# A graph network's third layer: the pass that scores the edges goes on in eight strands, its q rows spread by two wide operations a step

## What is computed

```
q = (x @ Wq_w + Wq_b)[dst]                       # per edge, by target node
k_base = (x @ Wk1)[src] + k_rel[edge_type] + Wk_b
score_base = sum(q * k_base, axis=-1)
scores = (score_base[:, None] + q @ v_rule.T) * scale      # E x 4
... softmax over edges of one (type, target), mean over rules: attn_mean
proj = einsum('nd,rdo->nro', x, W_r)             # 6250 x 32 x 128
msg = proj[src, edge_type] * attn_mean[:, None]
out = segment_sum(msg, dst) + bias
```

## Time and profile before

| what | us |
|---|---|
| timed runs | 8304.05, 8308.06, 8335.11 (median 8308.06) |
| profiled execution | 8250.15, span of its instructions 8248.4 |
| VectorE busy over the span | 3976.9 (48%) |
| GpSimd busy over the span | 5188.7 (63%) |
| TensorE, ScalarE busy | 893.5, 698.3 |
| line 2110, the gathers of this pass | 781.4 busy, 387.6 idle before them |

### The profile page before, as it was taken

One profiled execution on the slowest core, in us unless ns is written; L12 is line 12 of the kernel. 1 busy time (PEld: TensorE's weight loads), 2 busy tenths in 40 slices (PEclk: granted clock), 3 DMA queues, 4 the chain that ended last, 5 costly groups with the idle time before them and its releaser, 6 DMA issues. The chain is left out here.

```text
span 8248.4 us, 28229 instructions
## 1 busy us (share of the span) xinstructions
PE 893.5 (11%) x3512; PEld 557.4 (7%) x3512; DVE 3976.9 (48%) x9781; ACT 698.3 (8%) x1673; POOL 5188.7 (63%) x5178
## 2 busy tenths in 40 slices
PE   7500000000000000000025654000000001000000
PEld 5500000000000000000012221000000001000000
DVE  8974456023434443343335666666333335454536
ACT  0021111000000010000013332000000003000002
POOL 0067763766767657677755666662767766676774
PEclk9999755555555555555557887555555555555555
DMA  2080001013333323232225776331323331333332
GB/s 49 1 325 2 2 1 25 15 20 84 95 95 99 96 88 107 85 103 88 90 79 184 260 247 213 105 104 38 93 85 93 95 95 54 85 102 87 100 87 65
DMA packets 302982, 771.14 MB, mean 93 GB/s; under 512 B 125644, under 2 KB 135938, under 8 KB 289482
## 3 DMA queue, kind: packets, MB, share of 16 engines
q0 software_dynamic: 166224, 282.97, 14.8%
q1 hardware_dynamic: 118356, 375.36, 12.4%
q10 hardware_dynamic: 18210, 111.02, 3.5%
HBM read 357.59 MB, written 411.37 MB: 93 GB/s over the span
## 5 line engine op out<-in xcount | busy, mean ns | idle before, releaser
L1797 POOL DMA_INDIRECT first_sj<-scores,first_atdst x784 | 799.6, 1020 | 690.9 <-POOLq L59 430.9
L846 POOL DMA_INDIRECT l2z_rows<-proj,l2z_idx x784 | 791.6, 1010 | 427.5 <-issue 242.5
L2110 POOL DMA_INDIRECT l2s_krow<-table_k,l2s_idx x784 | 781.4, 997 | 387.6 <-issue 263.3
L846 POOL DMA_INDIRECT l3z_rows<-table,l3z_idx x784 | 797.5, 1017 | 327.1 <-issue 236.7
L846 POOL DMA_INDIRECT l1z_rows<-table,l1z_idx x784 | 783.4, 999 | 333.1 <-issue 241.5
L846 POOL DMA_INDIRECT l0z_rows<-table,l0z_idx x784 | 773.2, 986 | 331.0 <-issue 233.9
L822 DVE SCALAR_TENSOR_TENSOR l2z_acc<-l2z_acc,g_dokeep,l2z_msg 128x128 f32<-128x128 f32 x784 | 278.3, 355 | 655.5 <-DVE l2z_acc L822 322.7
L822 DVE SCALAR_TENSOR_TENSOR l1z_acc<-l1z_acc,g_dokeep,l1z_msg 128x128 f32<-128x128 f32 x784 | 277.8, 354 | 571.6 <-DVE l1z_acc L822 276.5
L2065 PE MATMUL l2s_bank<-l2o_wr,l2s_fed 128*128 128x512 f32 x800 | 418.4, 683 | 300.6 <-ACT l2s_fed L2089 204.5
L2047 DVE SCALAR_TENSOR_TENSOR l2s_qrow<-l2s_qrow,g_dokeep,l2s_zrow 128x82 f32<-128x82 f32 x1568 | 366.6, 300 | 171.9 <-DVE l2s_qrow L2047 117.4
L822 DVE SCALAR_TENSOR_TENSOR l0z_acc<-l0z_acc,g_dokeep,l0z_msg 128x128 f32<-128x128 f32 x784 | 277.3, 354 | 277.0 <-DVE l0z_acc L822 146.0
(11 more groups left out here) (571 smaller groups left out, 3627.4 us busy)
## 6 DMA issues: line engine op xcount, KB each, us to landing
proj<-l2s_proj ACTq DMA_DIRECT2D x100, 1024.0 KB
spread_q<-prep_zero SPq DMA_DIRECT2D x98, 656.0 KB
l2s_zrow<-spread_q SPq DMA_DIRECT2D x98, 656.0 KB
prefix<-l3z_acc SPq DMA_DIRECT2D x98, 520.0 KB
prefix<-l0z_acc SPq DMA_DIRECT2D x98, 512.0 KB
prefix<-l1z_acc SPq DMA_DIRECT2D x98, 512.0 KB
prefix<-l2z_acc SPq DMA_DIRECT2D x98, 512.0 KB
first_sj<-scores,first_atdst POOLq DMA_INDIRECT x784
```

What stands on the lines that cost most here:

```text
L846: nc.gpsimd.indirect_dma_start(out=rows[:, r, u, :], out_offset=None, in_=table, in_offset=bass.IndirectOffsetOnAxis(ap=idx[:, k * U + u:k ...
L1797: nc.gpsimd.indirect_dma_start(out=sj[:, j, :], out_offset=None, in_=g.scores0, in_offset=bass.IndirectOffsetOnAxis(ap=at_dst[:, j:j + 1], ...
L2110: nc.gpsimd.indirect_dma_start(out=krow[:, h, u, :], out_offset=None, in_=g.table_k, in_offset=bass.IndirectOffsetOnAxis(ap=idx[:, h, u:u ...
```

## The change

The 784 columns of a partition are cut into eight strands of 98 columns (`STRANDS`, `STRIDE`), and step k works on column k of all eight strands at once. The recurrence then goes over 98 steps, each on 8 x 164 columns, by two wide operations (times `keep`, plus the row of `spread_q`) in place of sixteen narrow ones per eight columns. Each strand needs its first row, so eight first q rows are gathered, not one. `krow` is a ring of six steps; GpSimd waits for the product of six steps ago (`used`). `zrow` is a ring of three double steps: 49 loads of 8 x 2 columns each, in 1024 pieces of 1312 bytes, each waiting for the sum of the step that frees its place (`summed`). All indices are converted at once at the start. `base` and `qv` are written with a stride of 98 columns. On ScalarE and TensorE the work is the same; the waits lose their extra instruction, and the last column stands in the loop.

```
+STRANDS = 8
+STRIDE = NC // STRANDS
+KRING, ZRING, ZSTEPS = 6, 3, 2
...
+        def step(ap, k):
+            return ap.rearrange("p (c j) -> p c j", c=STRANDS)[:, :, k]
...  VectorE, before
-                for i in range(STEPS):
-                    chain.loop(i, 2 * (2 * U + 6))
-                    for h in range(2):
-                        c = bass.ds(i * 16 + 8 * h, U)
-                        hold(eng, zgot[h], i * 16 + 16)
-                        for u in range(U):
-                            for f in range(2):
-                                if u:
-                                    chain.until(1)
-                                w = slice(f * QROW // 2, (f + 1) * QROW // 2)
-                                prev = qrow[:, h, u - 1, w] if u else qrow[:, 1 - h, U - 1, w]
-                                chain.add(v.scalar_tensor_tensor(qrow[:, h, u, w], prev, order.keep[:, bass.ds(i * 16 + 8 * h + u, 1)],
-                                                                 zrow[:, h, u, w], ALU.mult, ALU.add))
-                        chain.until()
-                        hold(eng, got[h], i * (16 * U) + 16 * U)
...  VectorE, after
+                v.tensor_copy(first[:], step(g.dst[:, 0:NC], 0))
+                v.tensor_copy(idx[:], g.src[:, 0:NC]).then_inc(asked, 1)
+                eng.wait_ge(begun, 16 * STRANDS)
+                for k in range(STRIDE):
+                    h, m = k % 2, k // ZSTEPS
+                    if k % ZSTEPS == 0:
+                        eng.wait_ge(zgot[m % ZRING], 16 * (m // ZRING + 1))
+                    chain.add(v.tensor_tensor(pick[:], bc_mid(g.iota[:, 0:TYPES], STRANDS), bc_last(step(g.type[:], k), TYPES), ALU.is_equal))
+                    chain(v.tensor_tensor(qrow[:, h], qrow[:, 1 - h], bc_last(step(order.keep[:], k), QROW), ALU.mult))
+                    v.tensor_tensor(qrow[:, h], qrow[:, h], zrow[:, m % ZRING, :, k % ZSTEPS], ALU.add).then_inc(summed, 1)
+                    eng.wait_ge(summed, k + 1)
+                    eng.wait_ge(got[k % KRING], 16 * STRANDS * (k // KRING + 1))
+                    v.tensor_tensor(prod[:], krow[:, k % KRING], qrow[:, h, :, 0:D], ALU.mult).then_inc(used, 1)
+                    chain.add(v.tensor_tensor(pick[:], pick[:], qrow[:, h, :, D:D + TYPES], ALU.mult))
+                    chain.add(v.tensor_copy(qv[:].rearrange("p a (c j) -> p c j a", c=STRANDS)[:, :, k], qrow[:, h, :, D + TYPES:QROW]))
+                    eng.wait_ge(used, k + 1)
+                    chain.add(v.tensor_reduce(part[:, 0], prod[:], AX, ALU.add))
+                    chain.until(2)
+                    chain(v.tensor_reduce(part[:, 1], pick[:], AX, ALU.add))
+                    chain(v.tensor_tensor(step(base[:], k), part[:, 0], part[:, 1], ALU.add))
...  GpSimd, after
+                for c in range(STRANDS):
+                    nc.gpsimd.indirect_dma_start(out=qrow[:, 1, c, :], out_offset=None, in_=g.table_q,
+                                                 in_offset=bass.IndirectOffsetOnAxis(ap=first[:, c:c + 1], axis=0)).then_inc(begun, 16)
+                for k in range(STRIDE):
+                    if k >= KRING:
+                        hold(pool, used, k - KRING + 1)
+                    for c in range(STRANDS):
+                        j = c * STRIDE + k
+                        nc.gpsimd.indirect_dma_start(out=krow[:, k % KRING, c, :], out_offset=None, in_=g.table_k,
+                                                     in_offset=bass.IndirectOffsetOnAxis(ap=idx[:, j:j + 1], axis=0)).then_inc(got[k % KRING], 16)
...  SyncE, after
+                z = g.spread_q[0:EP, :].rearrange("(p c j) w -> p c (j w)", c=STRANDS, j=STRIDE)
+                for m in range(STRIDE // ZSTEPS):
+                    if m >= ZRING:
+                        sp.wait_ge(summed, ZSTEPS * (m - ZRING + 1))
+                    sp.dma_start(zrow[:, m % ZRING].rearrange("p c j w -> p c (j w)"),
+                                 z[:, :, m * ZSTEPS * QROW:(m + 1) * ZSTEPS * QROW]).then_inc(zgot[m % ZRING], 16)
```

More of the change, by code:

```diff
@@ L2021, in scores_and_projections @@
         bank = [s.ps(f"bank{k}", [P, wide]) for k in range(banks)]
-        vs, fi, fg = s.sem("vs"), s.sem("fi"), s.sem("fg")
+        vs, asked, begun, summed, used = (s.sem(n) for n in ("vs", "asked", "begun", "summed", "used"))
         feed, multiplied, copied = s.sem("feed"), s.sem("multiplied"), s.sem("copied")
         stored = [s.sem(f"stored{h}") for h in range(2)]
-        idx_ready, got, zgot, used = ([s.sem(f"{n}{h}") for h in range(2)] for n in ("idx", "got", "zgot", "used"))
+        got = [s.sem(f"got{r}") for r in range(KRING)]
+        zgot = [s.sem(f"zgot{r}") for r in range(ZRING)]
+        def step(ap, k):
+            return ap.rearrange("p (c j) -> p c j", c=STRANDS)[:, :, k]
         with s.block() as block:
@@ L2065, in column @@
                         nc.tensor.matmul(bank[k][:], fed[:], wr[:, k * wide:(k + 1) * wide], start=True, stop=True).then_inc(multiplied, 1)
-                for i in range(STEPS):
+                for i in range(steps):
                     hold(pe, feed, i + 1)
@@ L2090, in _ @@
+                        lo = i * (TYPES * D) + h * part_wide
+                        act.dma_start(table[:, lo:lo + part_wide], proj[:, h * part_wide:(h + 1) * part_wide]).then_inc(stored[h], 16)
+                    if i < steps:
+                        nc.scalar.copy(fed[:], xT[:, i + 1, :]).then_inc(feed, 1)
                 for h in range(2):
                     act.wait_ge(stored[h], 16 * NB)
-                    for k in range(4 * h, 4 * h + 4):
-                        act.wait_ge(multiplied, 8 * (NB - 1) + k + 1)
-                        nc.scalar.copy(proj[:, k * wide:(k + 1) * wide], bank[k][:]).then_inc(copied, 1)
@@ L2106, in _ @@
[L2106 to L2111 removed]
+                pool.wait_ge(asked, 1)
+                for c in range(STRANDS):
+                    nc.gpsimd.indirect_dma_start(out=qrow[:, 1, c, :], out_offset=None, in_=g.table_q,
+                                                 in_offset=bass.IndirectOffsetOnAxis(ap=first[:, c:c + 1], axis=0)).then_inc(begun, 16)
```

63 lines of the change are left out of this document (11 added, 52 removed).

## The result

The changed kernel takes 8389.97 us (median of 4 runs, 8375.78 to 8392.75) where the kernel before, run beside it, takes 8321.02 (8304.05 to 8335.11). The ratio is 1.008, 95% interval 1.0053 to 1.0107: 69 us slower, where 21 us less were forecast, and 20 us above the upper end of the range.

A forecast was written before the change was run, and what follows sets the result against it. GpSimd's gather queue was taken as the bound. 979 (gathers) + 11 (start) + 127 (delays) + 18 (holes) + 10 (waits) + 10 (end) = 1155 us against 1176, 21 less: 8287 us, range 8215 to 8370.

The forecast's parts named there:

- Part 1: GpSimd's waits in the pass: with six ring steps, 10 us of 133 kept (0 to 30), its own holes stay.
- the 133 us: GpSimd's idle time before the change: 124 us waiting for VectorE's index lists, plus short waits booked as nobody's.
- GpSimd's own holes: Six holes in GpSimd's line, one at every 112th gather, 18 us, expected to stay with the number of gathers.
- Part 2: Gathers delayed by VectorE's two-input operations: 1.3 us a step, 127 us in all (69 to 206), mean gather 1.11 us.
- Part 3: VectorE's slow steps take 9.5 to 12.6 us against GpSimd's 11.5; the ring covers the difference, no further cost.
- Part 4: Other costs: 11 us at the start, 10 at the end; loads, ScalarE and TensorE nothing on the path.
- The small items: Eight first q rows 10 us, index conversion 0.57, end of pass 10 (5 to 40), loads nothing.
- The sum: From first q gather to VectorE's last operation of the pass: 1176 us before, 1155 after, 21 less.
- (b): Slower rival, chance 0.20: GpSimd never pauses long, VectorE's slow stretch never ends; 62 us more, 8370.
- (a): Fast rival, chance 0.22: gather delays 0.7 us a step, no waits for VectorE; 1083 us, 93 less, 8215.
- (c): Rival, chance 0.06: pieces of 1312 bytes come late, VectorE waits for them, the 133 us stay; 102 more, 8410.

The follow-up runs named there:

- the ring-of-two kernel: The changed kernel with its ring for k's rows cut from six steps to two: 0.9902 of before with slow stretches, 1.0099 without.

## Why the prediction was wrong, point by point

**Part 1, the ring of six.** Right in kind, larger than said: nothing is left of the 133 us where 10 were kept, and nothing of the 18 of GpSimd's own holes, which were to stay and went with the ring.

**Part 2, the wide operations.** Right: a mean gather of 1.098 us was measured, 1.11 forecast; (1.098 - 0.947) x 784 = 118 us in place of 127, and narrow operations bring it back to 0.997. The Trainium skill, page "SBUF — State Buffer", section Who interferes with whom, has the loser wait for the whole of an instruction with two inputs. By that rule halving the operations should have about halved their share; the trace shows 62 us, inside the 54 to 78 of the undivided ones, and the measurement decides.

**Part 3, the slow stretches.** The slow step was to take 9.5 to 12.6 us and took 12.60. What I had in a row as "1.4 per instruction" I used for VectorE alone. It also didn't last: VectorE has eleven such steps, between 4660 and 4800 us, and else waits for rows.

**Part 4, the step that failed.** "TensorE is idle from 5200 on, long before the last gather: nothing." That cover of 465 us was costed at nothing because it was there, and I didn't ask what made it. (I had also written that TensorE loses waits by the change; it loses none, its program is the same in both kernels.) In the earlier trace rows TensorE runs 183 matmuls in 150 us; but it pays up to 1.4 us an instruction in a slow stretch as VectorE does, 45 us a column, and it was GpSimd's pauses of before that kept its average at 14.2 (behind each of the 13 of 4 us or more a column of 8.7 to 11.6 us starts). The change takes the pauses away: 50 columns then need more than the pass has, and the rest, 19 columns at 9 us, is done when GpSimd is through. Price: 162 - 4 (the step over the end took 4.4 us before) = 158 us. The small items held: 10.1 us for the first q rows (11), 6.3 at the end (10), no wait for a load that shows.

**The sum.** From the first q gather to VectorE's last operation of the pass it is 1115.6 us (4427.2 to 5542.8), where 1155 were forecast and 1176 were before: 60 us gained, not 21. Adding the 158, the stage is 98 longer. Had the cover held, the forecast would have been 40 us too careful.

**The rivals.** (b) had the mechanism, "GpSimd never pauses long, and the slow stretch never ends", and put it on VectorE, where it didn't happen. VectorE's slow stretch ended at 4800 us although GpSimd had no idle time over 0.31 us (products, a step apart each):

```profile
4787.30 1.22 DVE L2049 TENSOR_TENSOR l2s_prod<-l2s_krow,l2s_qrow 128x1024 f32<-128x1024 f32 x1 [0.57 <-DVE l2s_qrow L2046]
...
4799.50 1.22 DVE L2049 TENSOR_TENSOR l2s_prod<-l2s_krow,l2s_qrow 128x1024 f32<-128x1024 f32 x1
...
4808.72 1.22 DVE L2049 TENSOR_TENSOR l2s_prod<-l2s_krow,l2s_qrow 128x1024 f32<-128x1024 f32 x1
...
4815.51 1.22 DVE L2049 TENSOR_TENSOR l2s_prod<-l2s_krow,l2s_qrow 128x1024 f32<-128x1024 f32 x1
```

What ended it the trace doesn't say. Eleven slow steps of 12.6 us against 11.2 of GpSimd's gathers (1099.2 / 98) are 15 us of delay, which the ring covers. (b) came near in its total (62 us more, 8370) for the wrong engine, which was luck; a chance of 0.20 for the mechanism was too little, since the earlier trace rows shows the end of a slow stretch right behind a pause. (a) had it right that no wait for VectorE is left, but the gathers' delays were 118 us where it had 69: 1116 lies between its 1083 and the forecast's 1155. The Trainium skill, page "Runtime: NRT & Kernel Launch", section Instruction fetch mechanics, from which (a) took its second reason, has refills in sequence hidden: the traces without slow stretches agree with it, and those with them don't contradict it: a packet of 16 KB on an instruction queue takes 0.9 to 1.1 us in the changed kernel's pass with slow stretches and 0.9 to 1.2 without, and there are seven of them in the whole pass. So fetching instructions doesn't show as what costs 1.4 us for each; what opens a stretch stays open. (c) fell: the ring-of-two kernel has the same loads.

What the prediction couldn't know is the second condition, and there its sum fails for another reason: the waits that pay for the wide operations (133 us) are 24 us there with the holes, so the price of part 2 stands alone.

## What to carry to other kernels

When a change removes the pauses of one engine, look for every engine that was late and recovered in them, those off the critical path too: work that ends 465 us early can owe that to the idle time you remove. Where engines have slow stretches, count instructions per unit of work, not busy time, and find what ends a stretch; a short, cheap pause of the busiest engine (6 us eight times) was worth some 135 us here (1.008 to 0.9916, from two groups of runs). It is pure cost where no engine has slow stretches (1.0245 with 24 pauses, against 1.0092 without). A deeper ring is a gain only as large as the waits it removes, and those should be measured in every condition in which the kernel runs.

## What the runs showed of the hardware

- With slow stretches, VectorE's and TensorE's semaphores rise as slowly as once in 1.4 us for each instruction, whatever its size: 9 instructions 12.60 us, 11 in 15.4, 15 in 20.99, a bank's 4 in 5.6, a half column's 16 in 22.40. Shorter intervals of 0.7 occur in the kernel before.
- TensorE's long columns end within a few us of an idle time of GpSimd of 4 us or more, in 65 of 73 cases. While GpSimd gathered without a break, 25 of 28 columns took 30 us or more; VectorE's slow stretch ended in the same pass without such an idle time.
- Matmul records can stand close together (16 in 9.90 us) while their semaphore rises once in 5.6 us. What the consumer loses is in its own idle time; the releaser named there was a DMA of another pass or "issue".
- The same program took 11% less in three groups of runs (7426 to 7449 us against 8314 to 8322), without one slow stretch, once on the very chip that showed them in another group.
- A gather's hold-up by two-input operations of VectorE is the same in both conditions (1.098 and 1.093 us with the wide ones, 0.997 and 0.991 in the kernel before).
